# Projection stage: the layer normalisation moves from VectorE to ScalarE, the values copy from ScalarE to VectorE, and twelve loads are issued one per block

## The reference

```python
mod = (_silu(L0_c) @ L0_wmod).reshape(L0_c.shape[0], 6, 1, -1)
sa, ca, ga, sb, cb, gb = (mod[:, 0], ...)
h = _layernorm(x, axis=-1) * (1 + ca) + sa        # (x - mean) / sqrt(var + 1e-5)
q, k, v = projections of h, 16 heads of 16; half of each q and k is rotated (RoPE)
scores = q @ k^T / 4, causal;  att = softmax(scores);  y = (att @ v) @ Wc
x = x + ga * y
```

## Time and profile before

| | us |
|---|---|
| median of 3 runs (2460.43 to 2464.82) | 2460.52 |
| the profiled execution | 2460.86 |
| its span, first to last instruction | 2459.1 |
| TensorE busy | 2306.0 |
| VectorE busy | 1894.2 |
| ScalarE busy | 1655.1 |
| GpSimd busy | 764.1 |

### The profile page before, as it was taken

How to read it: one execution, slowest core, us unless ns; L and a number is a source line. 1 busy time by engine, 2 the same in 40 slices (tenths; PEclk the granted TensorE clock), 3 DMA queues, 4 the chain that set the end, 5 groups by cost and what they waited for, 6 DMA issues and landing times. The chain is left out here.

```text
span 2459.1 us, 84837 instructions
## 1 busy us (share of the span) xinstructions
PE 2306.0 (94%) x34552; PEld 1509.9 (61%) x34553; DVE 1894.2 (77%) x3219; ACT 1655.1 (67%) x2983; POOL 764.1 (31%) x894
## 2 busy tenths in 40 slices
PE   6988589999999999999999999999989789899998
PEld 4555245655655555555555655555458789899997
DVE  5888688888898898898898898898638843555664
ACT  1666356777778877788788787888865555455554
POOL 2445401121211211211211211211215667676554
PEclk8999699999999999999999999999999899999999
DMA  5698563443434434434434433321247755565665
GB/s 170 198 249 234 155 110 89 88 112 83 100 97 98 99 96 99 93 96 101 99 94 103 99 90 85 77 59 38 69 144 229 255 122 117 111 131 106 97 104 88
DMA packets 224655, 287.95 MB, mean 117 GB/s; under 512 B 29463, under 2 KB 177975, under 8 KB 223927
## 3 DMA queue, kind: packets, MB, share of 16 engines
q1 hardware_dynamic: 185308, 235.53, 38.2%
q0 software_dynamic: 31872, 41.30, 9.8%
q10 hardware_dynamic: 7136, 6.32, 0.8%
HBM read 143.37 MB, written 138.81 MB: 115 GB/s over the span
## 5 line engine op out<-in xcount | busy, mean ns | idle before, releaser
L243 DVE TENSOR_REDUCE mxc<-ps 128x2 f32<-128x1024 f32 (+4 forms) x1168 | 1283.6, 1147 | 170.1 <-PE ps L230 98.0
L1201 ACT ACTIVATE probs<-ps 128x512 f32<-128x512 f32 (+1 forms) x2240 | 1165.5, 589 | 328.8 <-PE ps L1153 311.6
L1169 PE MATMUL ps<-probs,vs 128*32 128x512 f32 (+3 forms) x5120 | 601.4, 529 | 5.7 <-issue 4.8
L230 PE MATMUL ps<-ks,qs 96*32 96x512 bf16 (+13 forms) x7040 | 496.7, 346 | 38.3 <-DVE mxc L243 20.6
L1153 PE MATMUL ps<-qs,ks 99*32 99x512 bf16 (+3 forms) x7040 | 511.9, 351 | 7.9 <-ACT probs L1201 4.3
L230 PEld LDWEIGHTS ps<-ks,qs 96*32 96x32 bf16 x7040 | 211.0, 97 | 269.8 <-DVE mxc L243 117.1
L1081 POOL TENSOR_SCALAR_AFFINE_SELECT probs<-probs 128x512 f32<-128x512 f32 x256 | 161.2, 637 | 600.7 <-ACT probs L1201 599.5
L1153 PEld LDWEIGHTS ps<-qs,ks 99*32 99x32 bf16 x7040 | 213.0, 96 | 169.0 <-ACT probs L1201 83.4
L1930 PE MATMUL ps<-x_t,w_at 128*128 128x128 f32 x1968 | 244.9, 279 | 0.0
L2061 POOL DMA_INDIRECT out<-ys,idx x120 | 192.5, 1604 | 142.7 <-DMA out<-ys,idx 89.7
L1930 PEld LDWEIGHTS ps<-x_t,w_at 128*128 128x128 f32 x1968 | 234.6, 195 | 0.0
(11 more groups left out here) (175 smaller groups left out, 2311.5 us busy)
## 6 DMA issues: line engine op xcount, KB each, us to landing
ks<-k_parts SPq DMA_DIRECT2D x66, 256.0 KB
qs<-q_parts SPq DMA_DIRECT2D x66, 256.0 KB
xs<-slot_x SPq DMA_DIRECT2D x126, 131.0 KB
v_ones<-vout SPq DMA_DIRECT2D x64, 256.0 KB, 3.6
vs<-v_ones SPq DMA_DIRECT2D x64, 256.0 KB, 3.2
attn_t<-o_sb SPq DMA_DIRECT2D x64, 256.0 KB, 2.9
slot_x<-zero SPq DMA_DIRECT2D x48, 262.0 KB, 2.6
q_parts<-parts SPq DMA_DIRECT2D x96, 128.0 KB, 2.5
```

The lines of the kernel that those rows point to most:

```text
L230: ins = pe.matmul(o[at_q, h, 0:n], qs[0:SROWS, h0 + h, i * P + at_q.start:i * P + at_q.stop], ks[0:SROWS, h0 + h, 512 * c:512 * c + n], st ...
L243: return dve.tensor_reduce(mxc[:, h0:h0 + nh, i, c], unit_view(ps, u, at), AX_X, ALU.max)
L1169: ins = pe.matmul(o_ps[SLOT * g:SLOT * (g + 1), lo:QJ], vs[:, r, j, SLOT * g:SLOT * (g + 1)], probs[:, (NKT * r + m) % NPB, g, 0:QJ - lo], ...
L1201: act.activation(probs[:, (NKT * r + m) % NPB, h0:h0 + nh, 0:QJ - lo], st_view(r, s), ACT.Exp, scale=DH ** -0.5).then_inc(exp_done, 1)
```

## The change

Three things change, all in `project`. VectorE no longer normalises x: it computes `nmr`, minus the mean times `rstd`, a 128x4 instruction, and ScalarE normalises with four activations of 128x256 (`normalise`), which scale by `rstd` and add `nmr`; they stand in ScalarE's turn between `modulate` and `copies`. VectorE also waits for the earlier block's normalisation before it overwrites `rstd`. The values copy goes from ScalarE's `copies` to a stage of VectorE's own (`values`), between `rotate` and `split`, with its waits. And SyncE issues the twelve loads one per block, from the sixth block on, with two ahead of the stores of the last block.

```diff
@@ -270,14 +270,14 @@
         cos, sin = sb("cos", [P, T]), sb("sin", [P, T])
         xin = sb("xin", [P, BPS, TPB, C])
         stats, mv = sb("stats", [P, TPB, 6]), sb("mv", [P, TPB, 2])
-        std, rstd = sb("std", [P, TPB]), sb("rstd", [P, TPB])
+        std, rstd, nmr = (sb(n, [P, TPB]) for n in ("std", "rstd", "nmr"))
         h_t = sb("h_t", [P, 2, KC, BLK])
         raw = sb("raw", [P, 2, 2, NM, BLK])
         rot, turned = sb("rot", [P, 2, BLK]), sb("turned", [P, 2, 2, BLK])
         parts = sb("parts", [P, 2, 3, 2, NM, BLK], BF16)
         vout = sb("vout", [P, 2, TPB, H, SLOT])
-        tab_ld, norm_step, std_done, hn_done, tr_done, ht_done, ones_done = (
-            sem(n) for n in ("tab", "norm", "std", "hn", "tr", "ht", "ones"))
+        tab_ld, norm_step, std_done, scale_done, hn_done, tr_done, ht_done, ones_done = (
+            sem(n) for n in ("tab", "norm", "std", "scale", "hn", "tr", "ht", "ones"))
         qk_done, v_done, copy_done, vcopy_done, rope_step, cos_done, hi_done, sub_done, mid_done, low_done = (
             sem(n) for n in ("qk", "v", "copy", "vcopy", "rope", "cos", "hi", "sub", "mid", "low"))
         x_ld = [sem(f"x{j}") for j in range(BPS)]
@@ -371,9 +371,9 @@
                         for par in range(2):
                             sp.wait_ge(st_parts[par], NPART * BPS // 2 + 1 + NPART * (1 - par))
                     m = t - BPS - 1
-                    if 0 <= m < len(COMBOS):
-                        load_keys(sp, d, 0, m, g0["ks"], g0["ld"])
-                        load_queries(sp, d, 0, m, g0["qs"], g0["ld"])
+                    for i in range(max(m, 0), m + 1 if t < NB - 1 else 2 * len(COMBOS)):
+                        load = load_queries if i % 2 else load_keys
+                        load(sp, d, 0, i // 2, g0["qs" if i % 2 else "ks"], g0["ld"])
                     store(t // BPS, t % BPS)
                 for par in range(2):
                     sp.wait_ge(st_parts[par], NPART * NB // 2 + 1)
@@ -398,12 +398,11 @@
                 def norm_end(b, j):
                     t = BPS * b + j
                     dve.wait_ge(std_done, t + 1)
+                    if not isinstance(t, int) or t > 0:
+                        dve.wait_ge(hn_done, t)
                     dve.reciprocal(rstd[:, :], std[:, :]).then_inc(norm_step, 1)
                     dve.wait_ge(norm_step, NORM * t + 3)
-                    for n in range(TPB):
-                        ins = dve.tensor_scalar(xin[:, j, n, :], xin[:, j, n, :], mv[:, n, 0:1],
-                                                rstd[:, n:n + 1], ALU.subtract, ALU.mult)
-                    ins.then_inc(hn_done, 1)
+                    dve.scalar_tensor_tensor(nmr[:, :], mv[:, :, 0], -1.0, rstd[:, :], ALU.mult, ALU.mult).then_inc(scale_done, 1)
 
                 def rotate(b, j):
 
@@ -420,6 +419,14 @@
                     dve.wait_ge(rope_step, ROPE * t + 2 + 1)
                     dve.wait_ge(cos_done, t + 1)
                     dve.tensor_tensor(raw[:, par, :, 1, :], turned[:, par, :, :], rot[:, :, :], ALU.add).then_inc(rope_step, 1)
+
+                def values(b, j):
+                    t, par, n = BPS * b + j, j % 2, 2 * b + j // 2
+                    dve.wait_ge(v_done, t + 3)
+                    if isinstance(b, int) and b == 0 and j == 0:
+                        dve.wait_ge(ones_done, 1)
+                    dve.wait_ge(st_v[par], NV * n + 1)
+                    dve.tensor_copy(vout[:, par, :, :, 0:DH], vp.rearrange("p n (j h s) -> p (n j) h s", h=H, s=DH)).then_inc(vcopy_done, 1)
 
                 def split(b, j):
                     t, par = BPS * b + j, j % 2
@@ -481,7 +488,7 @@
                 dve.memset(g0["mxc"][:, :, :, :], -3e38).then_inc(head_set, 1)
                 dve.wait_ge(ld_small, 16 * 2)
                 dve.tensor_copy(k["mask_qk"][:, :], mask_in[:, :]).then_inc(head_set, 1)
-                staged(dve, (0, normed), (2, rotate), (3, split))
+                staged(dve, (0, normed), (2, rotate), (2, values), (3, split))
                 dve.wait_ge(head_set, 2)
                 for u in range(HEAD):
                     dve.wait_ge(g0["red_ready"], u + 1)
@@ -530,6 +537,13 @@
                     act.wait_ge(norm_step, NORM * t + 2)
                     act.activation(std[:, :], mv[:, :, 1], ACT.Sqrt, bias=k["eps"][:, :]).then_inc(std_done, 1)
 
+                def normalise(b, j):
+                    act.wait_ge(scale_done, BPS * b + j + 1)
+                    for n in range(TPB):
+                        ins = act.activation(xin[:, j, n, :], xin[:, j, n, :], ACT.Identity, bias=nmr[:, n:n + 1],
+                                             scale=rstd[:, n:n + 1])
+                    ins.then_inc(hn_done, 1)
+
                 def modulate(b, j):
                     t = BPS * b + j
                     if isinstance(b, int) and b == 0 and j == 0:
@@ -546,16 +560,11 @@
                     ins.then_inc(ht_done, 1)
 
                 def copies(b, j):
-                    t, par, n = BPS * b + j, j % 2, 2 * b + j // 2
+                    t, par = BPS * b + j, j % 2
                     for x in X:
                         act.wait_ge(qk_done, 2 * t + x + 1)
                         act.wait_ge(low_done, 2 * t + x + 1)
                         act.copy(raw[:, par, x], qk[:, NM * x:NM * (x + 1), :]).then_inc(copy_done, 1)
-                    act.wait_ge(v_done, t + 3)
-                    if isinstance(b, int) and b == 0 and j == 0:
-                        act.wait_ge(ones_done, 1)
-                    act.wait_ge(st_v[par], NV * n + 1)
-                    act.copy(vout[:, par, :, :, 0:DH], vp.rearrange("p n (j h s) -> p (n j) h s", h=H, s=DH)).then_inc(vcopy_done, 1)
 
                 def split(b, j):
                     t, par, n = BPS * b + j, j % 2, 2 * b + j // 2
@@ -576,7 +585,7 @@
                                           a[name]).then_inc(ld_up, 16)
                 act.wait_ge(ld_c, 16 * 3)
                 act.activation(c_sig[:, :], c_in[:, :], ACT.Sigmoid).then_inc(sig_done, 1)
-                staged(act, (0, norm), (1, modulate), (2, copies), (3, split), peeled=1)
+                staged(act, (0, norm), (1, modulate), (0, normalise), (2, copies), (3, split), peeled=1)
 
             @block.tensor
             def _(pe):
```

## The result

The changed kernel took 2514.48 us in the median of five runs (2510.26 to 2517.9). The kernel before, in five runs beside them, took 2464.82 (2460.43 to 2469.86). The ratio is 1.0197 [1.0186, 1.0208]: the change makes the kernel 2% slower. On the 2460.52 from which the forecast started, that ratio is 2509.0 us; the forecast was 2504.0, the range 2488 to 2514, and the median itself lies 0.5 above its upper end.

The account below looks back on a forecast made before the run. With no engine full, a loop of waits sets the projection's turn: 12.83+1.97+1.13 = 15.93 us. With the exposed head at the end, the barrier moves by 43.1: 2460.86+43.1 = 2504.0 us, range 2488 to 2514.

Parts of the forecast that it names:

- head: Attention's first units, at the projection's end: start only after the last load, then 14.6 us plus 0.55 for the first products.
- turns 3 to 14, less two requests of x: Main projection turns: 15.93 us each instead of 12.83, +29.7 for twelve; turns requesting no x save 0.43 each.
- last shuffle to SyncE's stores: End of projection: 11.17 us before, 12.3 with one more values copy, until stores of the last block but one begin.
- last two loads, issue to landing: Behind the stores of the last block but one: 0.64 us each to issue, then 5.5 to land.
- Normalisation, 1.97 and 2.07: On ScalarE between modulation and q and k copies: adds 1.97 us a turn, bounds 1.45 and 2.07.
- Values, 1.13: VectorE's values copy between rotation and subtraction: 1.21 us less 0.08 overlap adds 1.13 a turn.
- "`nmr` ... cost nothing": VectorE makes `nmr` where L404 started, at 115.70; ScalarE asks at 117.29, so it adds nothing to the turn.
- Setup, "2 us either way": Setup and turns 1 and 2: nothing taken beyond +1.1 for turn 2's values copy, with 2 us either way.
- Rival A: End of projection: late loads do not expose the head, only SyncE's 36.6 us remains, 2497.5 us; chance 0.14.
- Rival B: Turns 3 to 14: transfers set the pace, spreading loads gives back 7.5 us, 2453 us; chance 0.03.
- Rival C: Turns: VectorE's load sets the pace, each some 1.6 us shorter, 19 in twelve, 2442 us; chance 0.03.
- Rival D: Turns: TensorE idles and stays at its lower clock, which sets the turn, 84 us more, 2588 us; chance 0.03.

Follow-up runs that it names:

- e5: The changed kernel with ScalarE's normalisation behind its q and k copies instead of ahead of them; 2484.9 us, 1.0072 of the kernel before.
- e1: The changed kernel with the loads two per block again, so the last pair is issued blocks earlier; 2502.8 us, 1.0145 of the kernel before.
- e2: The kernel before with only the loads changed, to one per block as in the changed kernel; 2470.9 us, ratio 1.0011.
- e3: The kernel before with only the normalisation moved to ScalarE; values copy and loads as before; 2485.02 us, ratio 1.009.
- e7: The changed kernel with normalisation behind the q and k copies, values copied a block later while VectorE waits for `std`, loads of e9; 2464.97 us, 0.9983 of the kernel before.
- e9: The kernel before with one load in each of blocks 5 to 8 and two in each of blocks 9 to 12; 2468.55 us, ratio 1.0000.
- e6: The changed kernel with GpSimd's low part of k cut to 8 of 512 columns; 2502.96 us in one run, no ratio.

## Why the prediction was right, and what was mis-sized

Its mechanism holds: the turn is a loop of waits with no slack, both moves put work into it, and the late loads expose the head. The sum came out 5.8 us short at the barrier. That it was no further off is partly luck: turn 3 began 2.6 us earlier than forecast, and without that it would have been 8.4.

| step | predicted | measured | off |
|---|---|---|---|
| start of turn 3 | +1.1 | -1.5 | -2.6 |
| turns 3 to 14, less two requests of x | +28.8 | +34.6 | +5.8 |
| turn 15 to its shuffle, less its request | +2.0 | +2.8 | +0.8 |
| two tail turns | +2.3 | +2.2 | -0.1 |
| last shuffle to SyncE's stores | 12.3 | 13.3 | +1.0 |
| those stores | 7.7 | 7.7 | 0.0 |
| last two loads, issue to landing | 6.8 | 7.2 | +0.4 |
| head | 15.1 | 15.5 | +0.4 |

- **Normalisation, 1.97 and 2.07.** Measured 1.98 on the path and 2.07 by itself. Right; e5 shows that the place made the cost. Two readings beside it were not right. The lower bound of 1.45 was called a price for twice the elements, but `h_t` has the same 1024 per partition, in two instructions instead of four. And "both moves go to the slower engine" is what the rows say of the values alone: VectorE's normalisation took 2.98, ScalarE's 2.07. Where GpSimd was idle, in turn 3, VectorE's four took 1.38 and were the quicker ones.
- **Values, 1.13.** In the loop 5.70 from shuffle to subtraction is 4.57+1.13, to the hundredth; the copy took 1.22 against the 1.21 taken.
- **"`nmr` ... cost nothing".** This is the term that failed. The forecast gave `nmr` the start of L404 and no length. It starts there, but ends 1.87 later, with GpSimd's low part, and in the turn the first leg is 4.36 instead of 3.93. The path through subtraction, middle part, low part and `nmr` had overtaken the one through statistics, `std` and `h_t`: from the subtraction of turn 6 (122.12) to the normalisation of turn 7 it takes 6.63 us, where the other path takes 2.27+3.93 = 6.20. That explains the +5.8 as well: eleven turns 0.47 over 15.93 are 5.1, turn 3 (15.72, GpSimd idle) takes 0.2 back, and the 0.9 for requests of x that fall away is not returned, since `nmr` and not the request is waited for. In turn 15 that wait is 0.82, the +0.8. The kernel before showed the hold, in a row that the forecast passed over: of L404's four instructions the first took 2.02 us, beside GpSimd's low part (to 113.35+4.22 = 117.57), and the median of all 64 was 403 ns. VectorE's timeline, and GpSimd's:

```profile
115.70 2.02 DVE L404 TENSOR_SCALAR xin<-xin,mv,rstd 128x256 f32<-128x256 f32 x1
...
113.35 4.22 POOL L519 TENSOR_TENSOR parts<-raw,parts 128x1024 bf16<-128x1024 f32 x2 [4.63 <-ACT parts L568]
```

- **Setup, "2 us either way".** Turn 3 started 2.6 earlier than forecast, a little outside these bounds. Three kernels that are the same up to there differ by 2.2, so scatter can be most of this, which the forecast from one execution could not know; how much of it is, these runs don't show.
- **The end.** The +1.0 is the same collision. In the rows of the end above, VectorE's subtraction at 301.05 gets in between two instructions of GpSimd; the second of these takes 3.16 where the first took 2.12, and the stores wait for it. Landing took 5.4 and 6.5 where 5.5 was taken, the second 0.1 above the upper bound of 6.4.
- **Rival A** fell: the head was exposed, and e1 put the price of it at 9.7 against the 6.5 between the forecast and A.
- **Rival B** had its mechanism right: e2 gives the turns back 7.0 of the 7.5. But its condition, a loop that gains less than 0.62 a turn, was missed, and e2 shows that even then the end would have taken it back.
- **Rival C** fell: VectorE lost work, and e3's turns grew by 21.3 us.
- **Rival D** appeared without deciding. The windows of two turns, columns as in the earlier trace rows:

```profile
108.03:124.39 16.36, 14.34 (x53) 8.95 (x52) 11.73 (x18) 9.61 (x14) 6.59 (x3) 1.00 0.60 173
124.39:140.73 16.34, 11.47 (x33) 6.41 (x32) 11.71 (x18) 9.60 (x14) 6.57 (x3) 0.79 0.74 213
```

The second turn has a granted clock of 0.79 and the first of 1.00, and both take 16.3 us; matmul records are missing in the second, so the busy times are not compared. TensorE's timeline has the transposes of both turns:

```profile
114.53 1.10 PE L598 MATMUL ps<-ident,xin 128*128 128x128 f32 x8 [2.02 <-ACT xin L543]
130.88 1.97 PE L598 MATMUL ps<-ident,xin 128*128 128x128 f32 x8 [4.87 <-ACT xin L543]
```

After 4.87 us of idle time they took 1.97 instead of 1.10, and the turn had room for it. So not every turn began slow: turns 4 to 12 had a clock of 0.79, 0.90 or 1.00, and all took 16.34 to 16.45 us.

## What to carry to other kernels

Where no engine is full, find the loop of waits and cost every instruction by whether it stands inside it: the same two moves cost 39 us inside (e1) and nothing in idle time (e7 against e9). Give a new small instruction the wait that its predecessor in that slot shows, not its arithmetic. And before transfers are spread out, look at who needs the last one: e2's 7 us were all paid back.

## What the hardware showed that was not expected

A VectorE instruction of 128x4 took 0.16 us with GpSimd idle and 1.87 beside GpSimd's subtraction, and ended with it; with that subtraction cut down it took 0.16 again (e6). At the end of the projection it went the other way, and GpSimd's instruction was the longer one, 3.16 for 2.12. The Trainium skill, "SBUF — State Buffer", section "Who interferes with whom", has it as a rule: a VectorE instruction with two inputs in SBUF contends with a GpSimd instruction that reads SBUF, the ports that they share are an exclusive lock, and issue order decides which of the two blocks. The traces agree, with these numbers, in both directions.
